# Three small steps of LayerNorm and block scaling, moved from VectorE to GpSimd

## The reference, cut to what matters

```
x = x + 0.5 * ffn(layernorm(x))        # "f1"
x = x + attention(layernorm(x))        # "pj" is its LayerNorm and projections
x = x + 0.5 * ffn(layernorm(x))        # "f2", the same weights as f1

layernorm:  (x - mean) / sqrt(var + 1e-5)               over the 128 features
ffn:        blocks of 32 features: amax = max|x|, scale = 2^(floor(log2 amax) - 2) * fscale
            xs = x / scale, clipped to +-6, rounded to a 4-bit float grid, times scale, times W
attention:  16 heads of 8 features, 512 by 512 scores, softmax, times v
```

## Time and profile before

| what | value |
|---|---|
| timed runs, median (lowest to highest) | 546.12 us (543.88 to 546.65) |
| the profiled execution | 543.84 us |
| its span, first to last instruction | 542.0 us |
| busy: PE, DVE, ACT, POOL | 455.4, 439.3, 380.4, 228.5 us |
| share of the span: PE, DVE, ACT, POOL | 84%, 81%, 70%, 42% |
| instructions: DVE, POOL | 1004, 336 |
| granted PE clock, mean over the span | 0.956 of full speed |

### The profile page before, as it was taken

The page is one execution under the profiler, slowest core; times in us unless marked ns, Lnnn a source line. Parts: engine busy times, 40 slices in busy tenths (PEclk is TensorE's granted clock), DMA queues, the critical chain, the costliest instruction groups (busy, mean ns, idle before and its releaser), DMA issues.

```text
span 542.0 us, 8359 instructions
## 1 busy us (share of the span) xinstructions
PE 455.4 (84%) x2564; PEld 151.8 (28%) x2564; DVE 439.3 (81%) x1004; ACT 380.4 (70%) x746; POOL 228.5 (42%) x336
## 2 busy tenths in 40 slices
PE   2140799999979999999989998999899989998841
PEld 1120232332323332333233222323233323232211
DVE  6636789897999789987998799979997798898125
ACT  6557138687876788687877777878777786777730
POOL 8100047423755365536562665447543624012300
PEclk9985679999999999999999999999999999999995
DMA  5012411231122202231122212210322023200000
GB/s 163 20 48 85 137 41 51 86 95 50 29 91 73 84 31 79 70 101 49 50 89 89 70 51 89 90 66 24 103 74 90 23 76 100 60 2 2 21 1 19
DMA packets 27960, 34.86 MB, mean 64 GB/s; under 512 B 6278, under 2 KB 21260, under 8 KB 27916
## 3 DMA queue, kind: packets, MB, share of 16 engines
q1 hardware_dynamic: 26284, 33.94, 20.3%
q10 hardware_dynamic: 1632, 0.39, 0.3%
HBM read 21.34 MB, written 8.39 MB: 55 GB/s over the span
## 4 chain that ended last, share of the span: by engine, by line
PE 53%; DVE 27%; issue 7%; ACT 6%; POOL 3%; DMA 2%; SPq 1%; POOLq 0%; ACTq 0%; DVEq 0%
PE ot L1105 16%; DVE negmax L882 14%; PE sc L1092 14%; PE st L1081 12%; ACT probs L638 3%; PE misc L1030 3%; PE misc L1047 2%; PE misc L1070 2%; DVE stats_f L751 1%; DVE amax_f L774 1%; ACT feat_k L528 1%; PE misc L1055 1%; PE misc L1025 1%; DMA feat_k<-parts_k 1%; PE misc L1063 1%
## 5 line engine op out<-in xcount | busy, mean ns | idle before, releaser
L882 DVE TENSOR_REDUCE negmax<-sc 128x1 f32<-128x512 f32 x512 | 331.4, 682 | 50.7 <-PE sc L1092 50.1
L638 ACT ACTIVATE probs<-st 128x512 f32<-128x512 f32 x512 | 271.7, 602 | 80.2 <-PE st L1081 78.7
L1092 PE MATMUL sc<-feat_k,feat_q 96*128 96x512 bf16 x512 | 185.3, 391 | 14.7 <-DVE negmax L882 11.7
L1081 PE MATMUL st<-feat_q,feat_k 99*128 99x512 bf16 x512 | 158.1, 380 | 9.6 <-ACT probs L638 8.9
L1105 PE MATMUL ot<-probs,vfeat 128*32 128x512 f32 x1024 | 136.2, 604 | 1.1 <-ACT probs L638 1.0
L1092 PEld LDWEIGHTS sc<-feat_k,feat_q 96*128 96x128 bf16 x512 | 49.7, 97 | 162.3 <-DVE negmax L882 105.7
L1081 PEld LDWEIGHTS st<-feat_q,feat_k 99*128 99x128 bf16 x512 | 49.3, 98 | 82.6 <-ACT probs L638 55.9
L1014 PE MATMUL misc<-identb,xq_f 128*128 128x128 bf16 x64 | 6.8, 235 | 36.9 <-DVE xq_f L826 36.5
L406 POOL TENSOR_TENSOR rstd_f<-ve_f,nhalf 128x4 f32<-128x4 f32 x16 | 16.5, 1034 | 40.8 <-DVE nm_f L763 40.7
L447 POOL TENSOR_SCALAR maxparts<-negmax 128x16 bf16<-128x16 f32 x32 | 8.3, 258 | 57.6 <-DVE negmax L882 57.6
L1105 PEld LDWEIGHTS ot<-probs,vfeat 128*32 128x32 f32 x1024 | 20.2, 108 | 37.5 <-ACT probs L638 23.7
(11 more groups left out here) (134 smaller groups left out, 468.8 us busy)
## 6 DMA issues: line engine op xcount, KB each, us to landing
feat_q<-parts_q SPq DMA_DIRECT2D x96, 96.0 KB
feat_k<-parts_k SPq DMA_DIRECT2D x96, 96.0 KB
qkswap<-qkpre SPq DMA_DIRECT2D x32, 128.0 KB, 2.0
parts_q<-qkparts_q SPq DMA_DIRECT2D x24, 128.0 KB, 2.3
parts_k<-qkparts_k SPq DMA_DIRECT2D x24, 128.0 KB, 2.3
xres<-in_L_attn_x_dram SPq DMA_DIRECT2D x8, 256.0 KB, 5.5
out_dram<-xres SPq DMA_DIRECT2D x8, 256.0 KB, 2.5
feat_q<-maxrows ACTq DMA_DIRECT2D x32, 12.0 KB
```

The lines of the kernel that those rows point to most:

```text
L638: nc.scalar.activation(probs[:, s % US, j * S:(j + 1) * S], st[:, bank(2 * s + j), :], ACT.Exp, scale=SCALE).then_inc(exp_done, 1)
L882: nc.vector.tensor_reduce(negmax[:, g, j:j + 1], sc[:, bank(16 * g + j), :], AX.X, ALU.max, negate=True).then_inc(sc_maxed, 1)
L1081: nc.tensor.matmul(st[:, bank(2 * s + j), :], feat["k"][par][0:MROWS, h, kb * P:(kb + 1) * P], feat["q"][par][0:MROWS, h, :], start=True, ...
L1092: nc.tensor.matmul(sc[:, bank(16 * g + j), :], feat["q"][par][0:SROWS, h, t * P:(t + 1) * P], feat["k"][par][0:SROWS, h, :], start=True, s ...
```

## The change

Three steps of 4 and 16 columns are done by GpSimd in place of DVE: `ve` and `nm` (before `rstd`), and the product with `invf` (before xs). For the three hurried FFN passes the product stays on DVE and is put directly before its reader. The semaphores count accordingly: `stats` rises by 2 in place of 3 per LayerNorm, `rstd` by 4 in place of 2.

```diff
@@ gpsimd: rstd
-                pool.wait_ge(s["stats"], 3 * b + 3)
+                pool.wait_ge(s["stats"], 2 * b + 2)
                 if after(b):
                     pool.wait_ge(s["norm"], b)
+                nc.gpsimd.tensor_scalar(k["ve"][:, :], k["mv"][:, :, 1], EPS, None, ALU.add).then_inc(s["rstd"], 1)
+                nc.gpsimd.tensor_scalar(k["nm"][:, :], k["mv"][:, :, 0], -1.0, None, ALU.mult).then_inc(s["rstd"], 1)
+                pool.wait_ge(s["rstd"], 4 * b + 2)
                 nc.gpsimd.tensor_tensor(k["rstd"][:, :], k["ve"][:, :], nhalf[:, :], ALU.pow).then_inc(s["rstd"], 1)
-                pool.wait_ge(s["rstd"], 2 * b + 1)
+                pool.wait_ge(s["rstd"], 4 * b + 3)
@@ gpsimd: scale
+                pool.wait_ge(s["scale"], 5 * b + 4)
+                nc.gpsimd.tensor_scalar(k["amax"][:, 4, :], k["amax"][:, 2, :], invf[:, 0:1], None, ALU.mult).then_inc(s["scale"], 1)
                 pool.wait_ge(s["scale"], 5 * b + 5)
@@ vector: aggregate
-                dve.wait_ge(s["stats"], 3 * b + 2)
-                nc.vector.tensor_scalar(k["ve"][:, :], k["mv"][:, :, 1], EPS, None, ALU.add)
-                nc.vector.tensor_scalar(k["nm"][:, :], k["mv"][:, :, 0], -1.0, None, ALU.mult).then_inc(s["stats"], 1)
@@ vector: block_scales
-                elif step == 3:
+                else:
                     dve.wait_ge(s["scale"], a + 3)
                     nc.vector.reciprocal(m[:, 2, :], m[:, 3, :]).then_inc(s["scale"], 1)
-                else:
-                    dve.wait_ge(s["scale"], a + 4)
-                    nc.vector.tensor_scalar(m[:, 4, :], m[:, 2, :], invf[:, 0:1], None, ALU.mult).then_inc(s["scale"], 1)
@@ vector: scale (hurried passes only)
+                dve.wait_ge(s["scale"], 5 * b + 4)
+                nc.vector.tensor_scalar(k["amax"][:, 4, :], k["amax"][:, 2, :], invf[:, 0:1], None, ALU.mult).then_inc(s["scale"], 1)
```

More of the change, by code:

```diff
@@ L557, in norm @@
                 if half == 0:
-                    act.wait_ge(s["rstd"], 2 * b + 2)
+                    act.wait_ge(s["rstd"], 4 * b + 4)
                     if n == "pj" and after(b):
@@ L747, in stats @@
                     dve.wait_ge(x_attended, 2 * b + 2)
-                if after(2 * b):
-                    dve.wait_ge(s["rstd"], 2 * b)
+                if after(b):
+                    dve.wait_ge(s["rstd"], 4 * b)
                 for t in range(T):
@@ L756, in aggregate @@
                 k, s = bufs[n], LN[n]
-                dve.wait_ge(s["stats"], 3 * b + 1)
+                dve.wait_ge(s["stats"], 2 * b + 1)
                 for t in range(T):
@@ L798, in norm @@
                 k, s = bufs[n], LN[n]
-                dve.wait_ge(s["rstd"], 2 * b + 2)
+                dve.wait_ge(s["rstd"], 4 * b + 4)
                 if n != "pj" and b > 0:
@@ L938, in slot @@
                             if hurried(n, nb):
-                                for step in range(1, 5):
+                                for step in range(1, 4):
                                     block_scales(n, nb, step)
[L941 to L944, removed]
+                        for nb, _ in turns_of_batch(b, par, s, at["amax"] + 1, first):
+                            if not hurried(n, nb):
+                                block_scales(n, nb, 2)
                         for nb, _ in turns_of_batch(b, par, s, at["scale"], first):
```

## The result

The changed kernel took 541.18 us (median of 8 runs, 540.35 to 541.48), the kernel before, timed beside it, 544.77 us (8 runs, 543.77 to 546.73). The ratio is 0.9926, interval 0.9909 to 0.9944: 0.74% faster. The time lies in the predicted range; the gain is 3.6 us where 2.2 were forecast, and it passes the 0.5% that the likeliest case stayed under.

What follows compares the result with a forecast made beforehand. Neither PE nor DVE was taken to bound the whole; DVE stretches, filling and draining, and GpSimd waits could pay. 0.65 + 1.03 + 0.25 + 0.50 + 0.33 - 0.6 = 2.16 us gained, from 545.1 to 543 us; range 539.8 to 546.8.

Steps and rivals of the forecast that it cites:

- the likeliest case: The forecast itself for the whole kernel: 2.2 us gained, 543 us, 0.4% less; chance 0.50.
- The bound: Neither PE nor DVE bounds the whole; gains only in DVE stretches, filling and draining, and DVE or PE waits for GpSimd.
- Term 1: Four repeated DVE stretches plus 97 us: ve/nm pair worth 0, product 0.13 each, 0.65 us gained.
- Term 2: DVE stretch at 148 us: nm no longer meets GpSimd's L480 (0.90), plus product 0.13; 1.03 us gained.
- the rival on the port: The 148 us meeting goes but another like it appears elsewhere; gain 1.3 us, 544 us; chance 0.12.
- a sign of being wrong: Listed signs against the forecast, among them a batch's 57.4 us shrinking by more than 0.3.
- Term 3: Filling and draining: 0.25 at 65 us, 0.50 at 436 and 487, 0.33 at 499 gained; three bare LayerNorms lose 0.6.
- The cover: Repeated stretches: 0.35 us left between the end of xs on GpSimd and its DVE reader, so nothing lost there.
- The slower rival: GpSimd's row from split to xs becomes the wait of DVE's L837; 4.3 us slower, 549 us; chance 0.10.
- Full value: The pair of f2 counts in the repeated stretches too, 4 x 0.26 more; 3.2 us gained, 542 us; chance 0.28.

Runs made afterwards that it cites:

- the second profile: Both kernels, unchanged, profiled once more: the kernel before took 547.53 us, the changed kernel 541.06 us.
- the late pair: Kernel before with f2's ve and nm of batches 0 to 4 two row maxima later, still on DVE: 542.14 us, ratio 0.9906.
- the best version: Changed kernel with ve and nm of the four hurried LayerNorms back on DVE: 539.95 us, ratio 0.9866 against the kernel before.
- the test with one instruction more: Changed kernel with one extra 128x4 GpSimd addition between nm and the power in f2 of batches 1 to 4: 541.29 us.

## Why the prediction was right, and where its size was off

**The bound.** Right. Apart from the two that were not in the sum (below), only the DVE stretch, the filling and draining, and waits between DVE, PE and GpSimd paid; the PE stretch kept its 38.70 us.

**Term 1.** The pair was taken at 0 in the repeated stretches. Right for a free pair, up to 0.06: DVE now waits 0.19 for its scores, and putting the pairs back cost 0.05 to 0.06 each. The product was worth 0.14 for 0.13. What was left out is a wait that got shorter: L485 takes 1.16 in place of 1.20, as nm no longer meets it, and PE's wait for the split falls from 0.36 to 0.32. Five stretches gave 0.96 in the first profiles for 0.65. (The 0.26 of a pair is itself 0.02 low: the reduction of 268.38 starts 0.10 before the product's end, not 0.08. Nothing hangs on it.)

**Term 2.** The mechanism and the price were right, 1.08 for 1.03 at 148 us. The count was wrong, and this is the step that failed. It was said that nm was held there because it starts 0.02 behind L480, and, in the rival on the port, that "the four other stretches keep their places". The trace before had the counterproof: a free nm at the same 0.02 (20 ns at 257 us, 19 at 148 us, where nm was held). Where held and free look alike, the profile shows one toss, and each of five places can be lost in another run. The tosses are not independent: in three of the five traces every place was held. The kernel before lost one in its profiled run and five in the second profile, where the batch shrank by 1.09 us, more than the 0.3 that the prediction named as a sign of being wrong. Its 17 runs on one chip spread over 4.8 us, which 5 x 0.9 would nearly cover (how many were held in them was not seen), while the changed kernel, which cannot lose them, spread over 1.1. So the gain on a run is about 1.3 to 2.0 us and 0.9 for each pair held (by the late pair's 542.14 against the best version's 539.95 with 0.9 of bare LayerNorms put back; and by 6.46 - 5 x 0.9 in the second profiles). How many were held in the runs timed for the result was not seen; from their mean of 545.1 it is an estimate of two or three, at 542.9 (543.84 - 0.9) for none. That the gain came within 1.4 us of the forecast is in part luck: with five held, as in the second profile, it is 6.5.

**Term 3.** 65, 436 and 487 us came to 0.29, 0.33 and 0.29 for 0.25, 499 us to 0.24 for 0.33. The bare LayerNorms cost 0.58 and 0.35, together 0.93 for 0.6: nm was let follow ve at once, and it follows after 0.08 more; the best version confirms both places.

**The cover.** The working put 0.35 us between the end of xs and its reader; 0.04 were there, and the test with one instruction more found none. Product (0.34 for 0.27) and hand-over (0.08 between instructions that don't depend on one another) made the row on GpSimd 0.3 longer. The slower rival named 0.35 over the estimate as the point from which it decides: the change stands on that edge without having crossed it.

**The rivals.** Full value named the nearest time, 542, for a reason that the pairs put back on DVE refute. The port wait did not move: beside the attention work no instruction of DVE is held that was free before.

**Not in the sum.** The clock's earlier rise, 0.9 us, and PE's wait for feat_k at 448 us: 0.18 and 0.46 in the two profiles before, none in the two after, 0.51 in the best version. The first differs between two profiles of one kernel, and whether the change makes the earlier rise likelier was not tried; what sets the second was not tried either. Both stay open.

## What to carry to other kernels

Before counting a stall once because it shows once, look at the places where the same two instructions stand in the same distance and nothing happens: if held and free look alike, count them all, with a chance, and expect the runs to spread by up to that price times the number of places. They can all fall the same way in one run. A small step that collides can be cured by putting it earlier or later on its own engine; moving it to another one gave no more at the collisions here. And a small instruction put on an engine where nothing runs beside it costs its whole row, hand-over included: move only those that have cover.

## What the runs showed of the hardware

A start in the trace is not the grant of the port: at the same 0.02 us between L480 and nm, with L480 first each time, nm is held or it is not, and which it was shows in the durations (1.20 and 0.16, or 1.15 and 1.15). In nanoseconds the free ones lie at 13 to 20 and the held ones at 19 to 29.

Two small instructions that don't depend on one another start 0.08 us apart on DVE (263.56 and 263.64) and 0.31 on GpSimd (263.87 and 264.18), where they don't overlap. Yet a power on GpSimd that needed nothing from the instruction before it started 0.19 behind that (264.91 to 265.10).

The hold goes both ways. In the kernel with the late pair GpSimd's split at 499 us ran beside DVE's clip (GpSimd, then DVE), and its first step took 0.54 in place of the 258 ns of the earlier trace rows, although its start stands 0.07 us ahead of the clip's; PE's transposes there came 0.29 us later:

```profile
498.64 0.54 POOL L472 TENSOR_SCALAR maxparts<-negmax 128x16 bf16<-128x16 f32 x1
```

```profile
498.71 0.43 DVE L872 TENSOR_SCALAR xc_f<-xs_f 128x512 f32<-128x512 f32 x1 [0.56 <-POOL xs_f L449]
```
